# Third layer's edge phase: the carried queries and the exponentials of each half are put in PSUM by ScalarE

## The reference, cut to what matters

```python
q = ((src @ q_w.T + q_b) * scaling).reshape(n, H, HD)
k = (src @ k_w.T).reshape(n, H, HD)
v = (src @ v_w.T).reshape(n, H, HD)
w = jnp.einsum('ehd,ehd->eh', q[e_dst], k[e_src])
mx = jax.ops.segment_max(w, e_dst, num_segments=n)
ex = jnp.exp(w - mx[e_dst])
den = jax.ops.segment_sum(ex, e_dst, num_segments=n)
attn_w = ex / (den[e_dst] + 1e-16)
msgs = attn_w[:, :, None] * v[e_src]
agg = jax.ops.segment_sum(msgs, e_dst, num_segments=n)
```

## Time and profile before

| | |
|---|---|
| time, median of 3 runs | 5445.45 us (5445.11 to 5450.29) |
| profiled execution: time, span | 5450.11 us, 5448.4 us |
| VectorE busy, share of the span | 3728.0 us, 68% |
| GpSimd busy, share of the span | 3924.3 us, 72% |
| gathers of this phase (L1864), first and last start | 2926.7 us, 4153.9 us |

### The profile page before, as it was taken

How to read it: one execution, slowest core, us unless ns; L and a number is a source line. 1 busy time by engine, 2 the same in 40 slices (tenths; PEclk the granted TensorE clock), 3 DMA queues, 4 the chain that set the end, 5 groups by cost and what they waited for, 6 DMA issues and landing times. The chain is left out here.

```text
span 5448.4 us, 55911 instructions
## 1 busy us (share of the span) xinstructions
PE 1991.3 (37%) x9749; PEld 999.4 (18%) x9749; DVE 3728.0 (68%) x7733; ACT 2105.0 (39%) x5941; POOL 3924.3 (72%) x2991
## 2 busy tenths in 40 slices
PE   2699999999500000000011000000000556665664
PEld 1354444444300000000011000000000322222222
DVE  9676666665578888888876666666666665656665
ACT  0333333332328778778731000000000354454442
POOL 0688888887168777777725888888886188878774
PEclk9899999999755555555555555555555777777777
DMA  9555555555336666666643555555554123232232
GB/s 403 158 103 102 97 98 95 99 102 108 85 102 243 222 236 227 246 236 230 223 169 131 173 174 176 171 168 171 176 175 139 36 93 101 93 102 92 94 102 67
DMA packets 283514, 819.47 MB, mean 150 GB/s; under 512 B 63269, under 2 KB 178485, under 8 KB 271250
## 3 DMA queue, kind: packets, MB, share of 16 engines
q1 hardware_dynamic: 99250, 504.98, 25.1%
q0 software_dynamic: 171504, 252.10, 21.3%
q10 hardware_dynamic: 12528, 60.37, 2.7%
HBM read 368.73 MB, written 448.51 MB: 150 GB/s over the span
## 5 line engine op out<-in xcount | busy, mean ns | idle before, releaser
L1864 POOL DMA_INDIRECT arena<-table,arena x784 | 989.5, 1262 | 238.9 <-issue 238.9
L624 POOL DMA_INDIRECT tab<-arena x560 | 986.9, 1762 | 189.7 <-issue 147.3
L2353 POOL DMA_INDIRECT arena<-table,arena x676 | 824.1, 1219 | 206.6 <-issue 205.5
L746 PE MATMUL psum<-arena 128*128 128x512 bf16 (+1 forms) x4704 | 958.9, 359 | 0.0
L1514 PE MATMUL psum<-ident,arena 128*128 128x128 f32 x15 | 3.7, 428 | 2533.9 <-DVEq L1542 2533.9
L1287 POOL DMA_INDIRECT arena<-table,arena x588 | 719.8, 1224 | 189.4 <-issue 178.1
L2440 PE MATMUL psum<-arena 128*128 128x512 bf16 x2025 | 580.1, 455 | 290.6 <-DVE arena L2472 171.0
L1333 ACT ACTIVATE arena<-arena 128x128 f32<-128x128 f32 x1974 | 598.7, 387 | 186.1 <-DVE arena L1441 123.6
L1441 DVE SCALAR_TENSOR_TENSOR arena<-arena 128x512 f32<-128x512 f32 x728 | 544.9, 749 | 13.4 <-issue 1.2
L746 PEld LDWEIGHTS psum<-arena 128*128 128x128 bf16 x4704 | 436.4, 99 | 480.6 <-issue 36.7
L1514 PEld LDWEIGHTS psum<-ident,arena 128*128 128x128 f32 x15 | 2.7, 213 | 2534.6 <-DVEq L1542 2534.4
(11 more groups left out here) (408 smaller groups left out, 4595.2 us busy)
## 6 DMA issues: line engine op xcount, KB each, us to landing
rows<-arena SPq DMA_DIRECT2D x56, 3808.0 KB
arena<-seg_rows SPq DMA_DIRECT2D x112, 896.0 KB
rows<-arena SPq DMA_DIRECT2D x56, 1008.0 KB
seg_rows<-arena ACTq DMA_DIRECT2D x28, 1792.0 KB
rows<-arena SPq DMA_DIRECT2D x56, 896.0 KB
arena<-table,arena POOLq DMA_INDIRECT x2048
arena<-src_lanes SPq DMA_DIRECT2D x56, 448.0 KB
tab<-arena POOLq DMA_INDIRECT x560
```

The source lines that it names most:

```text
L624: eng.indirect_dma_start(out=m.tabs[j], out_offset=bass.IndirectOffsetOnAxis(ap=idx[g][:, k:k + 1], axis=0), in_=rows[g][:, k, 0:D], in_of ...
L746: t = eng.matmul(ps[:, c, 0:w], part[n // 2 % PAIRS][:, n % 2, :], hot[n % HOTS][:, lo:lo + w], start=False, stop=False, skip_group_check= ...
L1864: eng.indirect_dma_start(out=kv[k][:, j, :], out_offset=None, in_=m.table2, in_offset=bass.IndirectOffsetOnAxis(ap=idx[k][:, j:j + 1], axi ...
L2353: eng.indirect_dma_start(out=feat[h][:, j, :], out_offset=None, in_=m.table3, in_offset=bass.IndirectOffsetOnAxis(ap=idx[h][:, j:j + 1], a ...
```

## The change

`ex` (the exponentials, one buffer for each parity of halves) now lies in PSUM banks 0 and 1, and a new tile `query` in banks 4 to 7. ScalarE gets a new step, `keep_query`: when the 14 carries of a half are made, it copies that half's queries (1792 elements) from SBUF into `query`, and VectorE's first product reads them there. The second product and the two small ones read `ex` in PSUM. The state rows' exponentials are now made by ScalarE from the gap a second time, in place of a copy of `ex`. The chains (L1926, L1963, the scans) stay in SBUF. ScalarE's last turn is written out behind the loop, as it has no next half to copy at its end.

```diff
-        ex = [A(H2, COLS) for _ in range(2)]
+        ex = [m.psum[:, h, 0:H2 * COLS].rearrange("p (a t) -> p a t", t=COLS) for h in range(2)]
+        query = m.psum[:, 4:8, :].rearrange("p a (t f) -> p (a t) f", f=D)[:, 0:HALF, :]
...
+                def keep_query(i, k):
+
+                    eng.wait_ge(carried, carried_before(i, k) + HALF)
+                    eng.activation(query, q[k], ACT.Copy).then_inc(in_psum, 1)
+
                 eng.wait_ge(begun, 5)
                 for k in range(2):
                     stage_marks(k, edges(0, k))
-                with eng.Fori(0, LOOPS) as i:
+                keep_query(0, 0)
+
+                def turn(i, last):
                     for k in range(RING):
                         h = k % 2
...
                         eng.activation(ex[h], gap[h], ACT.Exp, scale=-1.0).then_inc(exped, 1)
                         stage_marks(k, edges(i, k + 2))
+                        if k + 1 < RING or not last:
+                            keep_query(*half(i, k + 1))
 
                         hold(eng, summed, sums_before(i, k) - SUMS2 + OLD2)
                         eng.activation(keeps[h], m.keep[:, edges(i, k)], ACT.Copy).then_inc(kept, 1)
 
                         eng.wait_ge(rows_free, i * RING + k + 1)
-                        eng.wait_ge(exped, i * RING + k + 1)
-                        eng.activation(rows[h][:, :, SUM:MAX], ex[h][:, :, 1:COLS].rearrange("p a t -> p t a"), ACT.Copy).then_inc(filled, 1)
+                        eng.activation(rows[h][:, :, SUM:MAX], gap[h][:, :, 1:COLS].rearrange("p a t -> p t a"), ACT.Exp, scale=-1.0).then_inc(filled, 1)
                         eng.activation(rows[h][:, :, MAX:R2], top[h][:, :, 1:COLS].rearrange("p a t -> p t a"), ACT.Copy).then_inc(filled, 1)
+
+                with eng.Fori(0, LOOPS - 1) as i:
+                    turn(i, False)
+                turn(LOOPS - 1, True)
...
                         eng.wait_ge(landed[k], 16 * HALF * (i + 1))
-                        eng.wait_ge(carried, carried_before(i, k) + HALF)
-                        ins = eng.tensor_tensor(prod, q[k], kv[k][:, :, 0:D], ALU.mult)
+                        eng.wait_ge(in_psum, i * RING + k + 1)
+                        ins = eng.tensor_tensor(prod, query, kv[k][:, :, 0:D], ALU.mult)
```

More of the change, by code:

```diff
@@ L1805, in layer2_edges @@
         begun = sem("buffers_begun")
-        carried = sem("queries_carried")
+        carried, in_psum = sem("queries_carried"), sem("queries_in_psum")
         scored, summed = sem("score_steps"), sem("sum_steps")
@@ L1825, in sums_before, with half @@
             return i * (RING * SUMS2) + (k + 1) * SUMS2
+        def half(i, k):
+            return (i + k // RING, k % RING)
         def edges(i, k):
@@ L1914, in _ @@
                 eng.wait_ge(q_first, 16)
-                def half(i, k):
-                    return (i + k // RING, k % RING)
                 def carry(i, k, j):
```

## The result

| | before | after |
|---|---|---|
| median of four runs, us | 5447.78 (5445.11 to 5450.29) | 5312.82 (5302.19 to 5315.62) |
| profiled execution, its span, us | 5450.1, 5448.4 | 5315.28, 5313.6 |
| first gather of the phase starts, last one starts, us | 2926.7, 4153.9 | 2915.4, 4010.8 |
| gathers' busy time, mean of one | 989.5 us, 1262 ns | 857.9 us, 1094 ns |

The ratio of the times is 0.9749, 95% interval 0.9732 to 0.9766: 135 us less. The forecast was 77 us less, and the low end of its range 5330. The kernel is faster by more than the range allowed.

What follows compares the result with a forecast made beforehand. GpSimd's gathers were taken to bound the phase. Freeing 2.0 us a half less 0.6 lost again gives 1.4 x 55 = 77 us: 5450.1 to 5373.1, or 5368 as median; range 5330 to 5412, chance 0.78.

Steps and rivals of the forecast that it cites:

- What bounds the phase: Third layer's edge phase: GpSimd's 784 back-to-back gathers set its length; 245 us of it could be won.
- The products' term: VectorE's two large products of each half stop holding gathers: 2.0 us a half, 110 us over 55 halves.
- PSUM as either input sets the gather free: A VectorE instruction with its first or second input in PSUM doesn't hold gathers; examples took 0.95 and 0.96 us.
- give-back: Freed requests meet the remaining small two-input instructions at another phase and lose some gain: 0.6 us a half.
- Bounds 0 and 1.85; I take 0.6: Limits and chosen value, in us a half, for gain lost again when freed gathers meet VectorE's small instructions.
- re-time the requests: Scans before VectorE's dense row of small instructions fix when held gather requests come, as today; so little is lost.
- The worst wait from the row's start: A request at the start of VectorE's dense row waits 3.2 us instead of 1.95, so 1.25 more.
- 5412 to 5437: Rival: small instructions take the gain back, saving only 0.15 to 0.6 us a half; chance 0.08.
- requests slip through: Rival: gathers find gaps in VectorE's dense row, up to 1.95 us more a half, under 5330 us; chance 0.06.
- The prices: PSUM reads cost VectorE nothing, products staying about 2.03 us; ScalarE's new copy takes 1.69 us a half.
- the tie at L1976: VectorE's first small instruction needs ScalarE's fills just as they finish: up to 0.3 us late.
- Idle ahead of the first product: VectorE's wait before each half's first product falls from 6.3 to about 4.9 us.

Runs made afterwards that it cites:

- experiment 2: Changed kernel with only the queries in PSUM, the exponentials back in SBUF: 5443.16 us, ratio 0.9977 to the kernel before.
- experiment 3: Changed kernel with only the exponentials in PSUM, the queries copied to SBUF: 5404.15 us, ratio 0.9910 to the kernel before.
- experiment 5: Changed kernel with the tiles `e` and `fwd`, read by the scans and L1181, in PSUM too: 5390.67 us, ratio 0.9883 to the kernel before.
- experiment 6: Changed kernel with the first product made twice, so later work comes 2 us later: 5377.79 us, ratio 0.9877 to the kernel before.
- experiment 1: Changed kernel, schedule kept, with queries and exponentials both back in SBUF: 5505.58 us, ratio 1.0084 to the kernel before.
- experiment 4: experiment 1 with one semaphore instruction added on VectorE directly ahead of the second product: 5445.13 us, ratio 0.9999 to the kernel before.
- experiment 10: Changed kernel with the phase's four engine loops written out: 5326.57 us, ratio 0.9793 to the kernel before.
- experiment 8: Changed kernel with VectorE's carries written straight into PSUM and ScalarE's query copy removed: 5501.17 us, ratio 1.0108 to the kernel before.
- experiment 12: Changed kernel with one semaphore instruction ahead of the fourth of the dense row's six pairs: 5241.83 us, ratio 0.9635 to the kernel before.
- experiment 7: Changed kernel with a semaphore instruction ahead of each of a half's 14 pairs of small instructions: 5581.64 us, ratio 1.0242 to the kernel before.
- experiment 17: experiment 16 with 48 semaphore instructions on VectorE ahead of the phase's first carry: 5281.63 us, ratio 0.9674 to the kernel before.
- experiment 18: experiment 8 with 48 semaphore instructions on VectorE ahead of the phase's first carry: 5224.95 us, ratio 0.9572 to the kernel before.
- experiment 16: experiment 12 with all four engine loops of the phase written out: 5407.82 us, ratio 0.9938 to the kernel before.

## Why the prediction was wrong in its size

- **What bounds the phase: right.** GpSimd's gathers, end to end, before and after. Shortening them shortened the span by the same amount.
- **The products' term: right.** It was 2.0 us a half, 110 us. By count, 245 us held before, less 110 for the dense row (52 halves of 1.95, two of 4.11) and 25 for the smaller holds, leaves 111 us, and the gathers that began in the two products were in fact held by 67 and 44 us; after, no gather that began in L1948 or L1964 took over 1 us. That PSUM as either input sets the gather free was right too, and it was right to let the trace decide against the statement of the Trainium skill ("SBUF — State Buffer", section "Who interferes with whom") that tensor_tensor didn't stall a DMA issued by GpSimd: experiments 2 and 3 each free the gathers from the product whose input they move.
- **The failed step is the give-back:** "Bounds 0 and 1.85; I take 0.6". It was not a loss but a gain of 0.33 us a half. The dense row holds 92 us instead of 110, the smaller holds 24 instead of 25, so 19 us came beside the 111, where 33 were to be lost. 111 + 19 = 130 of the 132 us of the phase; the other 2 are an undisturbed gather's 0.946 us instead of 0.949. With 0.6 replaced by -0.33 the prediction's own sum is 2.33 x 56 = 130, and its profiled execution's 5450.1 - 130 = 5320, where the one after took 5315.28.
- **Why the bound was wrong.** The prediction said, rightly, that the small instructions before the row re-time the requests; experiments 5 and 6 bear it out, since without two SBUF inputs in the scans and L1181 the holds lost their two sizes, while moving all of VectorE's work by 2 us left most of them (37 of 49 halves). But it used that only to say that little would be given back. A request arrives in a grid of small instructions: one pair later (0.54 us) it is held 1.41 instead of 1.95. In the kernel before, all 54 were at the earlier place (52 held by 1.95, two by 4.11), and so they are in experiments 1 and 4, where the first product still reads SBUF. Freed, half of them (27) fell on the later one. A bound of 0 from below needs a reason that excludes a gain, and there was none. The gain's size is in part luck: in experiment 10, the same tiles with the loops written out, only 10 requests fell on the later place, the held time was 2.39 us a half, and nothing was given back or gained.
- **Two slips in its working.** The worst wait from the row's start is 3.21 us from request to release, where today's is 2.08; it was set against 1.95, which is an excess over an undisturbed gather, so the bound is 1.1 and not 1.25. And of 5412 to 5437 some nine tenths, not three quarters, lie more than 0.2% below the kernel before. Neither decides the outcome.
- **A cost that the prediction didn't see, and that the change hides.** Its sum went from the holds of before straight to those of after, as if the new order of instructions held like the old one. Experiments 1 and 4 show that it doesn't. The section on the change says that no instruction moved on VectorE; a semaphore instruction did: the two waits ahead of the second product became one, ahead of the last carry. With both tiles in SBUF this makes the dense row and the second product one unbroken hold, 46 us in all. As the product reads PSUM, this never comes due. The sum was not hurt, but a reader who put only the queries in PSUM would have got experiment 2: 0.2% or 13 us (its slow stretch cost it another 13) instead of the 56 x 1.15 = 64 us that the first product alone held.
- **The rival "requests slip through"** gives the time, with "If the new phase finds such gaps in the dense row", and had 0.06. It named the right place but the wrong manner: no gather passes the dense row unheld (54 holds there before, 54 after); they are held for less.
- **The prices: right.** VectorE's products take 2024 and 2013 ns (expected about 2030 each), ScalarE's copy 1667 ns (1690), and the tie at L1976 came out as 12.6 us over 43 waits, 0.3 each. Idle ahead of the first product fell to 3.9 us a half rather than 4.9, which is the same missed 1 us.

## What to carry to other kernels

Where VectorE instructions hold GpSimd's gathers, find the unbroken rows of two-input instructions, not only the long ones: take one input of the long ones from PSUM, and try to cut a row of short ones with a single semaphore instruction (78 us here for one instruction a half), and look in the trace whether the gather was let in there. When an arrival is moved against a row of short instructions, give the change of its hold a range with both signs, of a pair or so. And when a variant that removes a wait turns out slower, look for idle put down to "issue" on another engine before dropping it: experiment 8 went from 5501 to 5225 us (ratios 1.0108 and 0.9572) by 48 idle instructions ahead of it, and in a kernel this tight any edit that moves code should be tried at two placements before its time is believed.

## What the runs showed of the hardware that was not expected

- In a row of small instructions with two SBUF inputs each, which start 0.27 us apart, a held gather is not let in at the end of one, only at the end of the row, and it ends 0.82 us on. A semaphore instruction of 0.02 to 0.05 us put between two of them lets it in: 5.05 us became 2.90 and 1.64 (experiments 1 and 4), and 2.90 became 1.30 (experiment 12). Not every boundary follows this: the two exceptions stand under experiment 4.
- A scalar_tensor_tensor with one input in PSUM doesn't hold gathers either, and it cuts a row as a semaphore instruction does: in experiment 8 each pair is one L1933 with a PSUM input and one L1970 with both in SBUF, and the held time is 0.13 us a half.
- VectorE can fall to about two instructions in 0.7 us for up to 75 us at a time, in some builds in every second half. In experiment 8 67 of SyncE's register instructions are slow as well, most of them in the same stretches, and none of ScalarE's and GpSimd's. Over the builds here it cost up to 305 us (experiment 7, the excess of 25 halves over 18 us). It went when 48 instructions were put ahead of the phase's work (experiments 17 and 18 against 16 and 8). Its cause is open; it was absent from the kernels before and after, and so had no part in the result itself.
